# A four-layer graph network on one core: straight copies of turned rows, two buffers for layer 0's products, and tile number loads in another place

## The reference, cut to what matters

```python
def _L0_gnn_ref(feat, W_src, b_src, W_dst, b_dst, attn, src, dst):
    el = feat @ W_src + b_src
    er = feat @ W_dst + b_dst
    e = jax.nn.leaky_relu(el[src] + er[dst], NEG_SLOPE)          # 0.2
    score = e @ attn
    smax = jax.ops.segment_max(score, dst, num_segments=N)
    ex = jnp.exp(score - smax[dst])
    ssum = jax.ops.segment_sum(ex, dst, num_segments=N)
    a = ex / ssum[dst]
    return jax.ops.segment_sum(el[src] * a[:, None], dst, num_segments=N)

def _L0_mix_ref(x, w_qkv, b_qkv, kln_g, kln_b, vln_g, vln_b, w1, b1, w2, b2):
    qkv = (x @ w_qkv + b_qkv).reshape(B, HW, HEADS, 3 * HEADC)
...
    k = _ln(k, kln_g, kln_b)
    v = _ln(v, vln_g, vln_b)
    kv = jnp.einsum('bhnd,bhne->bhde', k, v) / HW
    out = jnp.einsum('bhnd,bhde->bhne', q, kv)
...
    h = jax.nn.gelu(ret @ w1 + b1, approximate=False)
    return h @ w2 + b2 + bias

xn = _layernorm(x, axis=-1)
x = x + _L0_gnn_ref(xn, ...) + _L0_mix_ref(xn[None], ...)[0]
x = x + _L0_ffn_ref(_layernorm(x, axis=-1)[None], ...)[0]
...
```

## Time and profile before

| | us |
|---|---|
| median of 3 runs | 9476.93 |
| lowest, highest | 9470.9, 9477.66 |
| profiled execution, its own time | 9457.24 |
| its span | 9455.5 |
| mean granted clock of PE in it | 0.838 |
| busy: PE / PEld / DVE | 6205.5 / 4815.7 / 5310.6 |
| busy: ACT / POOL | 2033.8 / 4320.8 |
| layer 0's opening | 1049 to 1365 |
| layer 0's attention pass | 1378 to 2700 |

### The profile page before, as it was taken

How to read it: one execution, slowest core, us unless ns; L and a number is a source line. 1 busy time by engine, 2 the same in 40 slices (tenths; PEclk the granted TensorE clock), 3 DMA queues, 4 the chain that set the end, 5 groups by cost and what they waited for, 6 DMA issues and landing times. The chain is left out here.

```text
span 9455.5 us, 96395 instructions
## 1 busy us (share of the span) xinstructions
PE 6205.5 (66%) x28010; PEld 4815.7 (51%) x28010; DVE 5310.6 (56%) x14545; ACT 2033.8 (22%) x4839; POOL 4320.8 (46%) x4412
## 2 busy tenths in 40 slices
PE   0011249999987767776744555553984888886699
PEld 0000128888864456664533333342872677775466
DVE  7778358888855455554242222274114588887433
ACT  0000115555532300000220000022221233333322
POOL 0000016666667777777656777702001577772000
PEclk9999879999997888887867777775996777777799
DMA  0000113333310333333102333301871233331000
GB/s 14 5 1 1 35 58 90 90 90 91 90 41 10 95 108 105 105 105 86 15 19 78 105 105 105 102 4 28 311 263 39 80 98 97 99 99 43 12 14 21
DMA packets 405087, 698.69 MB, mean 74 GB/s; under 512 B 154168, under 2 KB 267809, under 8 KB 404071
## 3 DMA queue, kind: packets, MB, share of 16 engines
q0 software_dynamic: 206848, 480.28, 18.7%
q1 hardware_dynamic: 197726, 212.28, 7.0%
HBM read 633.06 MB, written 59.07 MB: 73 GB/s over the span
## 5 line engine op out<-in xcount | busy, mean ns | idle before, releaser
L737 POOL DMA_INDIRECT att_rows<-el_table,dst_order_row x1600 | 1556.7, 973 | 1410.2 <-POOLq L90 660.6
L714 PE MATMUL sum_sum<-sum_rows,sum_hot 128*125 128x256 f32 x3520 | 1215.7, 506 | 855.0 <-DMA sum_rows<-el_table,dst_order_row 462.2
L714 PEld LDWEIGHTS sum_sum<-sum_rows,sum_hot 128*125 128x125 f32 x3520 | 833.7, 248 | 1160.4 <-issue 812.2
L577 POOL DMA_INDIRECT dst_order_record<-records,dst_order_edge x784 | 806.5, 1029 | 404.1 <-issue 236.2
L642 POOL DMA_INDIRECT sum_rows<-el_table,dst_order_row x880 | 835.2, 949 | 295.8 <-issue 266.2
L642 POOL DMA_INDIRECT sum_rows<-rel_table,src_order_row x880 | 839.6, 954 | 274.9 <-issue 265.9
L664 DVE TENSOR_TENSOR gnn_acc<-gnn_acc,sum_sum 125x256 f32 x440 | 181.9, 413 | 1205.8 <-PE sum_sum L714 1201.7
L1217 PE MATMUL att_sum<-att_rows,att_hot 128*125 128x265 f32 x1440 | 475.5, 486 | 2.5 <-DVE att_rows L1108 2.4
L878 PE MATMUL att_found<-gnn_to_dst,att_hot_t 125*128 x1760 | 442.2, 395 | 37.5 <-issue 37.5
L902 PE MATMUL att_sum<-att_rows,att_hot 128*125 128x257 f32 x1760 | 437.4, 391 | 0.0
L940 ACT ACTIVATE att_rows<-att_rows,att_p 128x257 f32<-128x257 f32 x880 | 376.0, 499 | 7.1
(11 more groups left out here) (804 smaller groups left out, 13144.9 us busy)
## 6 DMA issues: line engine op xcount, KB each, us to landing
block_w<-in_L_ffn_W_dram SPq DMA_DIRECT2D x112, 512.0 KB, 6.2
block_w<-in_L_ffn_W_dram SPq DMA_DIRECT2D x56, 1024.0 KB
att_rows<-el_table,dst_order_row POOLq DMA_INDIRECT x1600
rel_table<-open_st SPq DMA_DIRECT2D x25, 784.0 KB
sum_rows<-rel_table,src_order_row POOLq DMA_INDIRECT x880, 2.7
sum_rows<-el_table,dst_order_row POOLq DMA_INDIRECT x880, 2.7
dst_order_record<-records,dst_order_edge POOLq DMA_INDIRECT x784, 2.3
pairs<-zeros SPq DMA_DIRECT2D x1, 7168.0 KB
```

The lines of the kernel that those rows point to most:

```text
L577: nc.gpsimd.indirect_dma_start(o["record"][:, k, :], None, o["records"], bass.IndirectOffsetOnAxis(ap=o["edge"][:, k:k + 1], axis=0)).then ...
L714: last = nc.tensor.matmul(slot(u), hot[u % HOTS_S][:, g, :], rows[l][:, g, :], start=(g == 0), stop=(g == G - 1))
L737: nc.gpsimd.indirect_dma_start(rows[l][:, g, 0:width], None, table, bass.IndirectOffsetOnAxis(ap=o["row"][:, k:k + 1], axis=0)).then_inc(s ...
```

## The change

Three things are changed.

1. In all openings `xT` is gone. ACT copies the turned rows from PSUM straight to XNT, with one copy in place of two, and PE's products read XNT. The semaphore between the copies is gone, and so is ACT's wait for the products of group i - 2.
2. Layer 0's opening has two `st` buffers in turn instead of one (`st_lanes` is left at 2). The memory for it comes from `sq`, which now lies in a spare part of the edge records' buffer.
3. In layer 0's attention pass, PE's load_tile stands between add_up and spread_scores instead of at the start of find; DVE's load_tile stands between lift and measure instead of at the start of raise_top.

```diff
@@ build_attend0
                 def raise_top(u):
 
-                    tile[u] = load_tile(dve, o, u)
                     old = nodes_of_unit(top, tile[u])
...
                     if u < N:
                         lift(u)
+                        tile[u] = load_tile(dve, o, u)
                         measure(u)
...
-                def find(u):
-
-                    tile = load_tile(pe, o, u)
+                def find(u, tile):
+
                     pe.wait_ge(s["hot_t_ready"], u + 1)
...
-                find(0)
+                find(0, load_tile(pe, o, 0))
                 for u in range(N + 2):
...
                         add_up(u - 2)
+                    if u + 1 < N:
+                        tile = load_tile(pe, o, u + 1)
                     if u < N:
                         spread_scores(u)
                     if u + 1 < N:
-                        find(u + 1)
+                        find(u + 1, tile)
@@ build_open
-        xn_s, xT = [sb(f"xn_s{l}", [R, GT, D]) for l in range(2)], [sb(f"xT{l}", [128, KB, GN]) for l in range(2)]
+        xn_s = [sb(f"xn_s{l}", [R, GT, D]) for l in range(2)]
...
                     act.wait_ge(s["flipped"], i + 1)
-                    if i >= 2:
-                        act.wait_ge(s["unit"], NUG // per * (i - 1))
-                    a.copy(xT[l][:].rearrange("p k (j x) -> p (k j) x", x=R), turned(wide[:])).then_inc(s["xt_ready"], 1)
-                    act.wait_ge(s["xt_ready"], i + 1)
-                    a.copy(XNT[:, :, i * GN:(i + 1) * GN], xT[l][:]).then_inc(s["xnt_ready"], 1)
+                    a.copy(XNT[:, :, i * GN:(i + 1) * GN].rearrange("p k (j x) -> p k j x", x=R), turned(wide[:]).rearrange("p (k j) x -> p k j x", k=KB)).then_inc(s["xt_ready"], 1)
...
-                            last = t.matmul(parts[n_u % 4][:, 0:n], xT[i % 2][:, k, j * R:(j + 1) * R], wk[k], start=(k == 0), stop=(k == KB - 1))
+                            last = t.matmul(parts[n_u % 4][:, 0:n], XNT[:, k, (i * GT + j) * R:(i * GT + j + 1) * R], wk[k], start=(k == 0), stop=(k == KB - 1))
@@ open0
-def open0(nc, c, m, I, dram):
+def open0(nc, c, m, I, dram, spare):
...
-             "gain": sb("gain", [R, 512]), "shift": sb("shift", [R, 512]), "hm": sb("hm", [R, 16 * GT]), "sq": sb("sq", [R, 16 * GT, 32]),
+             "gain": sb("gain", [R, 512]), "shift": sb("shift", [R, 512]), "hm": sb("hm", [R, 16 * GT]), "sq": spare[:, 0:16 * GT * 32].rearrange("p (n x) -> p n x", x=32),
...
-    build_open(nc, c, 0, m["X"], m["XN"], m["XNT"], loads, units, post, stores, kv, keep_blocks(c, 1.0 / NODES, m["KV"]), hand=(ACT.Sqrt,), st_lanes=1, pair=True)
+    build_open(nc, c, 0, m["X"], m["XN"], m["XNT"], loads, units, post, stores, kv, keep_blocks(c, 1.0 / NODES, m["KV"]), hand=(ACT.Sqrt,), pair=True)
@@ layer0
-        open0(nc, c, m, I, dram)
+        open0(nc, c, m, I, dram, by_dst["record"][0:R].rearrange("p c k -> p (c k)"))
```

More of the change, by code:

```diff
@@ L1430, in build_open @@
         bufs = [shared | {"xn_s": xn_s[l]} | ({} if tile_store else {"st": st[l % st_lanes]}) | {k: x[l] for k, x in w.items() if isinstance(x, list)} for l in range(2)]
-        names = ["loaded", "var", "std", "xn", "kept", "flipped", "xt_ready", "xnt_ready", "unit", "unit_out", "to_hand", "handed", "post", "kv_added", "chain", "passed"]
+        names = ["loaded", "var", "std", "xn", "kept", "flipped", "xt_ready", "unit", "unit_out", "to_hand", "handed", "post", "kv_added", "chain", "passed"]
         stored = [f"stored{l}" for l in range(TILE_LANES if tile_store else 2)]
```

## The result

| | before | after |
|---|---|---|
| median of 4 runs, us | 9473.92 | 9373.32 |
| lowest to highest | 9470.1 to 9477.66 | 9369.1 to 9377.57 |
| ratio, 95% interval | | 0.9894, 0.9877 to 0.9911 |
| profiled execution's span | 9455.5 | 9370.5 |
| first to last lift of layer 0's pass | 1306.4 | 1214.8 |

The kernel is 100.6 us faster (9473.92 − 9373.32), where 76.6 were forecast. 9373 lies under the range, which ended at 9384. The pass alone gives 1306.4 − 1214.8 = 91.6. (The first and last start of the lift are 1381.2 and 2687.6 before, 1379.6 and 2594.4 after.) The forecast gave it 67.9. Of the 27.0 by which the forecast of 9400.3 missed, 23.7 are the pass, 0.3 all that is outside it, and 3.0 come from the fourth run of the kernel before, which moved its median from 9476.93 to 9473.92.

The account below looks back on a forecast made before the run. The prediction took a loop through PE and DVE to bound layer 0's pass, and waits for products its opening. Gains of 67.9 (pass) and 8.7 (openings), 76.6 us together, took 9476.9 to 9400; range 9384 to 9442.

Parts of the forecast that it names:

- The loop: Layer 0's attention pass: score, spread, find and lift, through DVE and PE, set the period; 5.94 us would become 5.63.
- The 0.31 of the sum: Layer 0's pass: us saved per unit by moving PE's load from between spread and find, low end of 0.31 to 0.35.
- 219 × 0.31 = 67.9: Layer 0's pass: us gained in total, from find(1) to find(219), each standing behind a spread.
- DVE's floor: Layer 0's pass: DVE's work and own steps take 5.60 us a unit without its wait at lift, capping the gain at 0.34.
- DVE's load: 0: Layer 0's pass: moving DVE's load gains 0 us, hidden by make_hot in its old place and by lift in the new.
- Straight copies: 8.7: Openings: dropping the second copy shortens a group 1 wait by 1.24 us in seven of nine openings, 8.7 us in all.
- Two lanes: 0: Layer 0's opening: the second buffer gains 0 us, since PE's next products stay behind the kv step that waits for post.
- D: Rival: in layer 0's opening two lanes overlap products with post, 82 us more, 9318 us; chance 0.02.
- A: Rival: in layer 0's pass only the matmul rows' idle of 0.16 us a unit is gained, 9433 us; chance 0.12.
- B: Rival: PE's load was already hidden in layer 0's pass, so only the openings gain, 9468 us; chance 0.08.
- C: Rival: PE's load is exposed in its new place in layer 0's pass, +0.19 us a unit, slower at 9510; chance 0.07.
- the forecast's own place for the load: Layer 0's pass: PE's load would start with add_up's last weight load, about 1804.2, and end at 1804.7, just fitting.

Follow-up runs that it names:

- pe_load: Kernel before with only PE's tile number load moved ahead of the spread: 9376.7 us against 9467.8, ratio 0.9901.
- dve_load: Kernel before with only DVE's tile number load moved behind the lift: 9472.3 us against 9467.8, ratio 1.0002.
- two_behind: Kernel before with PE's tile number load made twice in its old place behind the spread: 9599.0 us in one run, beside 9462.3.

## Why the prediction was wrong

- **The loop** was the right one: score, spread, find, lift, with the load in it. The period fell because PE's load left it; DVE's load did nothing (`pe_load`, `dve_load`).
- **The step that failed** is the size of the gap that stays: "without the load find follows spread by 0.51 (spread's busy time, back to back) to 0.55". It is 0.43 (1801.82 − 1801.39). Where the second of two neighbouring instructions waits for nothing, these rows overlap: its start comes some 0.08 before the end of the first. The row of before says so: find's idle of 0.35 plus 0.08 is the 0.43 gained on PE, and in the earlier trace rows the turn, busy 0.63, has find 0.55 behind it. The 0.31 of the sum came from taking that 0.55 over to the spread, which is busy for 0.12 less; its other end, 0.35, came from the spread's full 0.51, without the 0.08 off. The term 219 × 0.31 = 67.9 measured 91.6.
- **DVE's floor** of 5.60 failed by the same overlap. The idle 0.34 was counted from the end of the copy ahead of the lift, but a lift that doesn't wait starts 0.07 to 0.08 before that end (1803.94 against 1803.86 + 0.15). From start to start, copy to lift, it was 0.50 before and is 0.08: 0.42 less, 5.94 − 0.42 = 5.52. I had even noted the overlap at L747 and L809, as a remark, and not used it. So "There is no more than 0.34 to be had" cut off the range at its low end; 219 × 0.42 = 92.0 would have been in place of 67.9.
- **DVE's load: 0.** Right. The measure starts 1.26 behind the lift's start with the load between them, 1.25 without.
- **Straight copies: 8.7.** The mechanism is right in the trace (1.34 where 1.37 was forecast). The size is in agreement, 100.6 − 91.6 = 9.0 as what the pass leaves of the whole and 6.3 (0 to 17) alone, but not shown to better than that, and layer 3's own opening shows none of its 1.24. One reading was off without consequence: POOL's scatter after `open2n` runs on to 6615.6 (its last start 6614.41), not 6612.6.
- **Two lanes: 0.** Right, and for the reason given: with PE's and ACT's order changed, some 85 us come (the forecast's D had put 82 on it).
- **Rivals.** A, by the matmul rows, fell: the idle of 0.16 there was far too small. B fell: the load was exposed. By the Trainium skill, "Perfetto Trace Analysis", Tensor Engine Instruction, a waiting instruction leaves the sequencer free to decode the next; here it did not get past the four transposes of the spread, the first of which waited (it stood there from 1801.8 to 1804.8), and of the one load 0.43, of the second 0.63, was in full view. The rule on computed ends in the same section of the Trainium skill agrees with the traces: the weight loads' starts told the gain (0.86 to 0.43), the matmul rows' idle of 0.16, a start less a computed end, did not.
- C fell, and the forecast's own place for the load was wrong with it. It had the load start with add_up's last weight load and end at 1804.7: "It fits, with little over." PE's queue runs far ahead instead: the load starts 2.7 us before the spread, and three fit.

## What to carry to other kernels

A gain that is read from an idle in a timeline should be counted from start to start, and against the start-to-start of the same two instructions somewhere without the wait: idle rows leave out the overlap of back-to-back rows, 0.08 here, which over 219 units was 18 of the 24 us that were missed in the pass. A gap taken from other instructions (the turn's 0.55 for the spread's) made the rest. In this kernel's queues a load of a register belongs ahead of an instruction whose semaphores are long set, not behind some that wait. And a second buffer brings nothing while one engine's written order still puts the next producer behind the consumer's last step: change the order with it.

## What the runs showed of the hardware

- PE's queue goes on past instructions whose semaphores are set: in the kernel before it had passed the eight products of place and add_up by 1801.8, before the first of them started at 1801.90, and three loads start from 2003.6 on, while place (from 2003.38) was running and add_up (from 2004.27) was still to come. It did not get past the spread's four transposes, the first of which waited for the score: it was at the spread at 1801.8 and at the load behind it at 1804.8, and both loads of `two_behind` start with the spread or later (2001.4 and 2002.0, the spread at 2001.39). It had passed eight products just before, so it is not that so many products do not fit; whether it can take a few that still wait is not shown.
- A load of a tile number with its check takes 0.63 us of PE's queue, while its three rows add up to 0.46 to 0.47.
- The four weight loads of the spread lie 0.43 from first start to the next instruction, four of the turn 0.55, though both have the same shape and a single one has a median of 187 ns in both. The reason is not shown.
- ACT's copy of turned rows from PSUM takes 1.20 to two stretches of 625 in XNT, the same as to one stretch of 1250 in xT.
